# Blocks of its own for the last tile of a fused attention and mixture-of-experts kernel, and its attention moved among the last blocks

## The reference: what is computed

```python
xn = layernorm(x)
# attention branch: linear, causal, 8 heads of 32
q, k = elu(xn @ Wq.T + bq), elu(xn @ Wk.T + bk)
u, v = silu(xn @ Wu.T + bu), silu(xn @ Wv.T + bv)
energy = (q @ k.T) * tril            # no softmax
att = (u * rms_norm(energy @ v)) @ Wo.T + bo
# expert branch: 8 experts, each token goes to one
top1 = argmax(xn @ Wg.T)             # Wg is 8 x 256
xhat = layernorm(xn)
e = top1                             # of each token
ffn = gelu((xhat * s[e] + b[e]) @ w1[e] + bb1[e]) @ w2[e] + bb2[e]
out = x + att + ffn
```

## Time and profile before

| what | value |
|---|---|
| median of three runs | 342.39 us (341.08 to 342.73) |
| the profiled execution itself | 343.99 us, its span from first to last instruction 342.2 us |
| TensorE matmul / weight load busy | 272.4 us (80%) / 231.8 us (68%) |
| VectorE, ScalarE, GpSimd busy | 206.7 (60%), 158.7 (46%), 186.5 us (54%) |
| mean granted TensorE clock | 0.908 of full speed |
| moved by transfers | 39.61 MB, 116 GB/s |

### The profile page before, as it was taken

The page is one execution under the profiler, slowest core; times in us unless marked ns, Lnnn a source line. Parts: engine busy times, 40 slices in busy tenths (PEclk is TensorE's granted clock), DMA queues, the critical chain, the costliest instruction groups (busy, mean ns, idle before and its releaser), DMA issues. The chain is left out here.

```text
span 342.2 us, 7905 instructions
## 1 busy us (share of the span) xinstructions
PE 272.4 (80%) x2912; PEld 231.8 (68%) x2912; DVE 206.7 (60%) x530; ACT 158.7 (46%) x296; POOL 186.5 (54%) x414
## 2 busy tenths in 40 slices
PE   2598997999799799799979955995776999697600
PEld 2487785888679588687868945884756878576400
DVE  6787492695488179369648914781486355555621
ACT  2358256545834845664492536351221656444200
POOL 6336666575577567547657641762474002756671
PEclk9999899899899989989989995999698899989955
DMA  7997013004003201300402100110004466889985
GB/s 262 316 345 219 3 63 124 2 33 156 0 2 112 77 2 62 124 3 18 162 9 64 63 1 2 61 63 2 1 17 131 130 187 212 267 231 344 302 286 173
DMA packets 33510, 39.61 MB, mean 116 GB/s; under 512 B 2481, under 2 KB 30657, under 8 KB 33473
## 3 DMA queue, kind: packets, MB, share of 16 engines
q1 hardware_dynamic: 30176, 30.69, 27.6%
q0 software_dynamic: 3072, 8.39, 7.8%
q10 hardware_dynamic: 224, 0.03, 0.1%
HBM read 20.23 MB, written 18.87 MB: 114 GB/s over the span
## 5 line engine op out<-in xcount | busy, mean ns | idle before, releaser
L1161 POOL DMA_INDIRECT x_in<-ys,rows x32 | 32.6, 1018 | 41.5 <-DMA ys<-y_blk 32.0
L581 ACT ACTIVATE e_neg<-ring,cols 128x512 f32<-128x512 f32 x32 | 22.0, 689 | 50.1 <-PE ring L245 50.1
L243 PE MATMUL ring<-xn_hi,w_hi 128*128 128x512 f32 x96 | 41.1, 429 | 1.8 <-DVE xn_lo L727 1.7
L742 DVE TENSOR_TENSOR energy<-ring,causal 128x512 f32<-128x512 f32 x64 | 39.5, 682 | 0.1
L245 PE MATMUL ring<-xn_hi,w_lo 128*128 128x512 f32 x96 | 39.3, 409 | 0.0
L244 PE MATMUL ring<-xn_lo,w_hi 128*128 128x512 f32 x96 | 39.2, 409 | 0.0
L1150 POOL DMA_INDIRECT xs<-x_in,rows x32 | 32.8, 1026 | 11.6 <-issue 7.3
L766 DVE TENSOR_TENSOR g<-ring,uT 128x512 f32<-128x512 f32 x16 | 11.0, 687 | 37.3 <-ACT sq L598 20.3
L365 PE MATMUL ring<-xT_blk,w_blk 128*128 128x128 f32 x156 | 26.3, 294 | 4.5 <-DVE w_blk L855 4.1
L286 PE MATMUL kv_bank<-v_tok,k_tok 128*32 128x32 f32 x480 | 9.0, 228 | 26.0 <-ACT k_tok L594 25.3
L757 DVE TENSOR_TENSOR state<-state,kv_bank 128x256 f32<-128x256 f32 x30 | 12.6, 421 | 26.4 <-PE kv_bank L286 25.0
(11 more groups left out here) (158 smaller groups left out, 759.7 us busy)
## 6 DMA issues: line engine op xcount, KB each, us to landing
xs<-blank SPq DMA_DIRECT2D x4, 1280.0 KB, 10.9
x_blk<-xs SPq DMA_DIRECT2D x20, 256.0 KB, 3.4
ys<-y_blk SPq DMA_DIRECT2D x20, 256.0 KB, 3.2
x_in<-in_x SPq DMA_DIRECT2D x8, 512.0 KB, 4.1
o<-in_x SPq DMA_DIRECT2D x8, 512.0 KB, 4.8
out<-o SPq DMA_DIRECT2D x8, 512.0 KB, 4.5
energy<-in_w_in SPq DMA_DIRECT2D x4, 256.0 KB, 4.5
energy<-in_w SPq DMA_DIRECT2D x1, 512.0 KB, 6.7
```

What stands on the lines that cost most here:

```text
L243: pe.matmul(bk, w_h(k), x_h(k), start=(first and k == 0), stop=False, skip_group_check=skip)
L581: act.activation(e_neg[t][:, :], bk[:, :], ACT.Exp, bias=vecs[:, col:col + 1]).then_inc(s[f"{w}_exp"], 1)
L742: dve.tensor_tensor(energy[:, t, m, :].rearrange("p (c n) -> p c n", c=CH), bank(f"s{t}{m}", n)[:, :].rearrange("p (c x) -> p c x", c=CH), ...
L1161: pool.indirect_dma_start(out=x_in[n % 3][:, c, :], out_offset=None, in_=ys[0:blocks * P, :], in_offset=bass.IndirectOffsetOnAxis(ap=rows[ ...
```

## The change

It has five parts.

1. Statistics first: VectorE takes the statistics of tile m at the start of the tick. GpSimd's `norm_scalars` runs a tick earlier, for tile m + 1, between `book(n)` and `scatter(n)`.
2. Four addresses a tick: `find_experts(i)` (the five small operations, now on one tile's 8 columns, with `which` holding addresses) runs in every tick, and `load_expert` loads two addresses behind it and two near the tick's end. The other 18 are loaded among the blocks, one per two blocks.
3. Tile 7 gets blocks of its own: after tile 6 all blocks are taken as closed (`CLOSED = 7`, `fill` set back). There are 46 blocks in 23 pairs. The first pair's load waits for the scatters of tiles 5 and 6, that of pair 14 for the scatter of tile 7.
4. Tile 7's attention: scores and masks stay ahead of the blocks. `attend`, the gating and the square sums, all in `kv_bank`, run at blocks 35 to 43 (`LATE` = 35), its output product behind the last block.
5. ScalarE copies every third block's result (`product_of`). `add_experts` comes at block 22 and then at every fifth block, no longer at 20 and every fourth.

```diff
-BLOCKS = B * T // P + NE - 1
-EARLY = CH * (TILES - 2)
-BACK = CH + NE - 1 + 9
+CLOSED = TILES - 1
+BLOCKS = CH * CLOSED + NE - 1 + CH * (TILES - CLOSED) + NE - 1
+LATE = CH * CLOSED + NE - 1
+BACK = CH + NE - 1 + 11
...
+        def product_of(k):
+            return (s["y_act"], k // 3 + 1) if k % 3 == 2 else (s["y_dve"], k - (k + 1) // 3 + 1)
...
@@ TensorE, among the blocks @@
+                i = TILES - 1
+                if k == LATE:
+                    attend(i, 0, kv_bank)
+                elif k == LATE + 3:
+                    pe.wait_ge(s["g"], 2 * i + 1)
+                    attend(i, 1, kv_bank)
+                elif k == LATE + 7:
+                    pe.wait_ge(s["g"], 2 * i + 2)
+                    square_sums(i, kv_bank)
...
@@ VectorE @@
+            def load_expert(k, n):
+                dve.wait_ge(s["expert"], n + 1)
+                weights_at[k] = dve.value_load(expert[k:k + 1, 0:1], min_val=0, max_val=(NE - 1) * WROW)
...
@@ VectorE, tick @@
+                if norm_next:
+                    norm_stats(m)
                 elu(n, "k", 0, bank("k0", i))
...
                 gated(i, 0, bank("att0", i))
-                if norm_next:
-                    norm_stats(m)
                 for c in range(CH):
                     logits_out(n, c, bank(f"v{c}", i))
                 choose_expert(n)
-                if i == TILES - 3:
-                    expert_of_blocks(TILES - 2)
-                if i >= TILES - 3:
-                    j = (i - (TILES - 3)) * EARLY // 2
-                    load_experts(j, j + EARLY // 2)
+                find_experts(i)
+                load_expert(CH * i, i)
+                load_expert(CH * i + 1, i)
                 gated(i, 1, bank("att1", i))
...
+                load_expert(CH * i + 2, i)
+                load_expert(CH * i + 3, i)
                 reciprocal(i)
...
@@ VectorE, among the blocks @@
+                if k == LATE + 2:
+                    gated(i, 0, kv_bank)
+                elif k == LATE + 5:
+                    gated(i, 1, kv_bank)
+                    square_sum(i)
+                elif k == LATE + 6:
+                    gated_lo(i, 0)
+                    gated_lo(i, 1)
+                elif k == LATE + 8:
+                    mean_square(i, kv_bank)
...
-                if k >= 0:
+                if k >= 0 and product_of(k)[0] is s["y_dve"]:
                     product_block(k)
+                if k == 5:
+                    find_experts(i)
+                if k >= 6 and k % 2 == 0 and CH * CLOSED + (k - 6) // 2 < BLOCKS:
+                    load_expert(CH * CLOSED + (k - 6) // 2, i)
...
@@ GpSimd, tick @@
-                if m < TILES:
-                    norm_scalars(m)
...
                 book(n)
+                if m + 1 < TILES:
+                    norm_scalars(m + 1)
                 scatter(n)
-                if n + 1 < TILES:
+                if n + 1 < CLOSED:
                     book_next(n)
+                elif n + 1 == CLOSED:
+                    pool.memset(fill[:, :], float(P)).then_inc(s["booked"], len(BOOK) - BOOK.index("spent"))
...
@@ SyncE, load_pair @@
-                    for b in (0, 1):
-                        sp.wait_ge(scattered[b], 64 * (TILES // 2))
+                    for n in (CLOSED - 2, CLOSED - 1):
+                        sp.wait_ge(scattered[n % 2], 64 * (n // 2 + 1))
+                if pair == CH * CLOSED // 2:
+                    n = TILES - 1
+                    sp.wait_ge(scattered[n % 2], 64 * (n // 2 + 1))
```

More of the change, by code:

```diff
@@ L70 @@
     "sq sq_sum ssq_pe ssq ms rms0 rms rinv g g_hi g_lo wo_pe added "
-    "past expert0 expert1 expert2 expert weights load_0 load_1 load_2 load_3 turned features hid_pe act y_pe y "
+    "past expert0 expert1 expert2 expert weights load_0 load_1 load_2 load_3 turned features hid_pe act y_pe y_dve y_act "
     "keep_0 keep_1 keep_2 keep_3 "
@@ L519, in last_tick @@
                 scores(i, 1, free1)
[L520 to L529, removed]
[L531 to L541 removed]
+            def free_block(k):
+                if k < BANKS:
+                    pe.wait_ge(s["masked"], 8 * (TILES - 1) + k + 2)
                 else:
[L543 removed]
+                    pe.wait_ge(*product_of(k - BANKS))
             for i in range(TILES - 1):
@@ L702, in act_program @@
                     hidden_block(k + 2)
+                if k >= 0 and product_of(k)[0] is s["y_act"]:
+                    product_block(k)
+                late_attention(k)
         def dve_program(dve):
@@ L843, in load_experts @@
-            def load_experts(j, k):
-                dve.wait_ge(s["expert"], 1 if k <= EARLY else 2)
-                for block_ in range(j, k):
-                    weights_at[block_] = dve.value_load(expert[block_:block_ + 1, 0:1], min_val=0,
-                                                        max_val=(NE - 1) * WROW)
+                begun = past[:, n, :]
+                dve.tensor_scalar(begun, first_block[:, n, :], block_col[:, :], None, ALU.is_le).then_inc(s["past"], 1)
+                dve.wait_ge(s["past"], n + 1)
@@ L1275, in sp_program @@
             sp.wait_ge(s["blank0"], 1)
-            for r in range(PAIRS // 5):
-                sp.dma_start(xs_pairs[5 * r:5 * r + 5].rearrange("k p j d -> p (k j) d"),
-                             blank[:, :].unsqueeze(1).to_broadcast([P, 10, D])).then_inc(s["blank"], 16)
+            for r in range(0, PAIRS, 5):
+                count = min(5, PAIRS - r)
+                sp.dma_start(xs_pairs[r:r + count].rearrange("k p j d -> p (k j) d"),
+                             blank[:, :].unsqueeze(1).to_broadcast([P, 2 * count, D])).then_inc(s["blank"], 16)
             for i in range(TILES - 1):
@@ L1292, in sp_program @@
                     keep_pair(pair)
-                    if 2 * pair >= BACK + 2 and (2 * pair - BACK - 2) % CH == 0:
-                        store((2 * pair - BACK - 2) // CH)
-            for n in range((2 * (PAIRS - 1) - BACK - 2) // CH + 1, TILES):
+                    stored = 2 * pair - BACK - 3
+                    if stored >= 0 and stored % 5 in (0, 1):
+                        store(stored // 5)
+            for n in range((2 * (PAIRS - 1) - BACK - 3) // 5 + 1, TILES):
                 store(n)
```

108 lines of the change are left out of this document (57 added, 51 removed).

## The result

| | before | changed |
|---|---|---|
| time, median of 4 | 341.74 us | 310.44 us (308.8 to 311.54) |
| ratio | | 0.9086, 95% interval 0.9027 to 0.9146 |
| profiled execution / its span | 343.99 / 342.2 | 308.8 / 307.1 |
| mean granted clock of TensorE | 0.908 | 0.983 |

A forecast was written before the change was run, and what follows sets the result against it. TensorE was taken as nearly full in ticks, with a mid-tick wait and low clock; address loads held ticks 5 and 6. First result at 240.7, blocks 66.2, tail 15.8 gave span 323.1, time 323.3 us; 8 in 10 for 312 to 334.

The forecast's parts named there:

- VectorE 2.5 us late: Start of ticks: two address loads and the statistics ahead of the first `e_neg`, 3.01 less 0.45 us slack.
- TensorE loses 1.7 us there: Attention in ticks 0 to 4: later masks make it start 9.9 us into the tick instead of 8.16.
- Of 2.2 us of waiting 0.3 come back as time: TensorE's wait before the state product: that product starts 22.2 us into the tick instead of 22.5.
- I take 0.7 of the 1.7 us of low clock as saved: TensorE in each tick: idle time breaks into smaller pieces, saving 0.7 of up to 1.7 us lost to low clock.
- the ticks gain in full: Rival for the ticks: five ticks gain 3.5 us each, 12.5 us less than forecast, 311 us; chance 0.09.
- The last tick: Masks to first result: first expert product at 253.6 instead of 265.50, 11.9 us earlier; first result at 240.7.
- The blocks: 45 intervals at 1.16 us, plus 0.6 for `find_experts`, 7.4 for additions and late loads, 6.0 for tile 7's attention: 66.2.
- the rival of slow blocks: Whole block stage runs at its second half's pace, 1.57 us per block: 10.5 us more, 334 us; chance 0.12.
- that of loads which set the pace: Rival for the blocks: loads of pairs near 10 us give 2.0 us per block, 347 us, slower than before; chance 0.03.
- The tail: Last copy to the end: store, fourth gather's issue and landing, addition and output take 15.8 us, 18.4 before.
- GpSimd's 2.7 us taken at 0: Scale and shift between booking and scatter delay GpSimd's scatters some 2.7 us; taken as no cost, else 2.7 per tick.

The follow-up runs named there:

- run with the statistics alone: Kernel before with only VectorE's statistics moved to the tick's start and GpSimd's scale and shift a tick earlier: 343.6 us against 363.4, ratio 0.9473.
- the alternating ticks: Ticks 1 to 4 of the changed kernel with statistics, scale and shift put back in mid-tick: 348.9 us against 362.6 for the kernel before, ratio 0.9626.
- six loads ahead: Changed kernel with pairs of blocks loaded six ahead instead of four, two more buffers laid over `e_neg`: 307.9 us, ratio 0.9039 to the kernel before.
- half the copies on ScalarE: Kernel with pairs loaded six ahead, ScalarE copying every second result instead of every third: 313.1 us, ratio 0.9161 to the kernel before.

## Why the prediction was wrong in size

- **"VectorE 2.5 us late" failed, and with it "TensorE loses 1.7 us there".** The lateness of `e_neg` is 1.24, that of the masks 0.95, and TensorE loses 0.72, in the second score group. The step that failed is charging the two address loads at the tick's end 1.23 us, ahead of an engine that still had 1.28 us of queued work. I measured the load where nothing covered it and used that price everywhere. The run with the statistics alone has the same stretched score group without the loads, and the runs with four loads in either place show both prices.
- **"Of 2.2 us of waiting 0.3 come back as time" failed with it.** The wait shrinks by 1.7, and the later masks take 0.7 of that back: the state product starts 21.4 us into tick 4, where it was 22.4 before (174.84 - 152.48) and I had 22.2. So 1.0 comes back. The full price of the mid-tick pair was not at fault: from the choice of expert to `g` 2.43 us pass (158.24 to 160.67), which is my 1.2 + 1.23.
- **"I take 0.7 of the 1.7 us of low clock as saved" failed.** The low clock vanished altogether, which is worth 1.1 us a tick (1.3 in the alternating ticks). The 1.7 was too high as well.
- Put together: wait -1.7, clock -1.1, masks +0.7, 2.1 us less a tick; the traces have 28.98 - 26.65 = 2.3. The forecast had 1.0. The truth in the ticks lies midway between it and the rival *the ticks gain in full* (3.5). That rival's 311 is the time by luck, only because the blocks and the first copy gave 5.9 us more as well.
- **The last tick** was right in mechanism; the first copy came 7.8 us after the masks and not 9.2. The first expert product starts 5.27 us after them, as forecast. In the earlier trace rows the copy trails that product by 3.9 us, at a granted clock of 0.60, now by 2.5 (227.04 to 229.53), at 1.00. The window before:

```profile
265.50:269.41 3.91, 3.91 (x21) 3.81 (x21) 0.00 (x0) 2.24 (x6) 0.00 (x0) 0.60 0.44 133
```

  These 1.4 us are not sure: in other runs with the same early start the copy comes 9.2 us after the masks, the changed kernel once more among them.
- **The blocks** were charged 66.2 and took 61.7. Up to block 22 it was 26.9 where I had 26.1. Mis-sized were the two terms behind it, 7.4 us for additions and late loads and 6.0 for the attention: together they took 8.1 (34.8 us from block 22 to 45, less 26.7). The 7.4 came from a window at clock 0.94, in which TensorE waited 2.9 us for pairs and 3.0 for weights; the changed kernel's last 31.7 us are at 1.00 and have 1.3 and 0.7, and 1.4 for ScalarE's features. How the 5.3 us divide between clock, waits and attention no run shows. So the rival of slow blocks is wrong, and so is that of loads which set the pace: the longest landing on the chain is 4.97 us.
- **The tail**, 15.4 for 15.8, and **GpSimd's 2.7 us taken at 0** were right. `rstd` takes 1.85 us at 150.20 and ScalarE's `xn` does not wait.
- The Trainium skill (DMA: Bandwidth & Descriptors, Latency and other measured facts) has a floor of about 600 ns for a register load. The price per load where nothing covers it agrees (0.615 us each in the earlier trace rows, 1.27 for the second two in mid-tick), though the load instruction itself takes 0.31 us; at the tick's end two loads cost 0, behind `xn_lo`. Of the page's grouping of four to amortize it this kernel shows nothing: four in a row in mid-tick take 2.68 us, where two take 1.41.

## What to carry to other kernels

A register load here cost its 0.6 us only where VectorE had nothing left to run, and nothing behind 1.28 us of queued work: read the price where it stands bare, then ask what lies in front of the new place. A wait on TensorE has to be priced twice, as idle time and as low clock behind it. Here the second (1.1 us per tick) went as a whole when the wait fell from 2.2 to 0.5 us; filling the wait with products of zeros measures it directly. An engine's lateness is not the loss of the engine that waits for it: take off each slack on the way.

## What the runs showed that I had not expected

- Discarded work on TensorE in a wait of 2.2 us shortened ticks from 28.98 to 27.89 us.
- The same wait of 2.36 us was followed by a low clock in every second tick only (0.95, 1.00, 0.95, 1.00). The wait for the first block's weights, 2.31 us, does the same from kernel to kernel. The first expert product in the changed kernel, and in the one with all copies on VectorE:

```profile
227.04 0.68 PE L375 MATMUL ring<-xT_blk,w_blk 128*128 128x128 f32 x4 [2.31 <-DVE w_blk L870]
```

```profile
228.15 1.20 PE L375 MATMUL ring<-xT_blk,w_blk 128*128 128x128 f32 x4 [2.31 <-DVE w_blk L870]
```

  The first copy comes 7.8 us after the masks in the first (7.8 also with six loads ahead), 9.2 in the second and in the changed kernel once more, 9.9 with half the copies on ScalarE. What decides between the two is not shown.
- Chips differ by 6% on the same kernel (341.7 and 363.4 us), with nearly the same duration for single instructions. The changed kernel, once more on a slower chip, has ticks of 28.1 us instead of 26.65, and 72.6 us from first to last copy instead of 61.7. Lines like these stand in the list of TensorE's waits there, and none with this releaser in that of the first trace:

```profile
PE ring L375 <- issue: 4.1, 3, 1.9
...
PE ring L327 <- issue: 1.5, 5, 0.3
```

  What the queue waits for in them is not shown. It is why ratios were taken inside a group, and why the differences in us of the slower chips should not be added to those of the others.
